# The one-hot table's weighting in the last layer of a decoder kernel moves from VectorE to GpSimd

## The reference

```
q = normalise(x @ w_q)                       # over all tokens, gamma and beta
sim = einsum("pbnhd,hkpd->pbnhk", q, keys)   # 2 halves, 8 heads, 64 keys
sx, ix = top_k(sim[0], 8);  sy, iy = top_k(sim[1], 8)
scores, pk = top_k(sx[..., :, None] + sy[..., None, :], 8)
indices = (ix * 64 + iy) picked by pk        # 8 heads x 8 picks per token
h = gelu(einsum("bnd,bnhkd->bnhk", x, down_embed[indices]))
h = softmax(scores) * h
out = einsum("bnhk,bnhkd->bnd", h, up_embed[indices])
```

## Time and profile before

| | us |
|---|---|
| median of 3 runs | 2479.22 (2472.06 to 2480.68) |
| the profiled execution, its own time | 2480.77 |
| its span in the trace | 2478.9 |
| PE busy | 1869.9 |
| DVE busy | 1342.1 |
| ACT busy | 747.7 |
| POOL busy | 243.8 |

### The profile page before, as it was taken

One profiled execution on the slowest core, in us unless ns is written; L12 is line 12 of the kernel. 1 busy time (PEld: TensorE's weight loads), 2 busy tenths in 40 slices (PEclk: granted clock), 3 DMA queues, 4 the chain that ended last, 5 costly groups with the idle time before them and its releaser, 6 DMA issues. The chain is left out here.

```text
span 2478.9 us, 35764 instructions
## 1 busy us (share of the span) xinstructions
PE 1869.9 (75%) x12618; PEld 1443.9 (58%) x12618; DVE 1342.1 (54%) x3974; ACT 747.7 (30%) x1470; POOL 243.8 (10%) x234
## 2 busy tenths in 40 slices
PE   6676776788888545887878766665878969969968
PEld 4555564656655434666666544444767757758757
DVE  3454445235433342555455534443499598697796
ACT  2231312132343323545545422230240330330420
POOL 1212212100000012000000001111010100000100
PEclk9888787867887776889888965557788989979979
DMA  2000000100000114877777511116000000000000
GB/s 84 1 17 17 0 17 0 52 6 26 25 17 1 48 55 156 295 269 279 280 249 262 189 37 34 34 34 256 9 1 1 18 1 6 14 1 6 14 1 9
DMA packets 90917, 174.74 MB, mean 70 GB/s; under 512 B 8224, under 2 KB 75296, under 8 KB 86052
## 3 DMA queue, kind: packets, MB, share of 16 engines
q1 hardware_dynamic: 90788, 173.05, 19.9%
HBM read 93.20 MB, written 79.69 MB: 70 GB/s over the span
## 5 line engine op out<-in xcount | busy, mean ns | idle before, releaser
L2122 PE MATMUL bank<-per_up,per_act_w 128*128 128x256 f32 x1024 | 256.3, 400 | 0.0
L95 PE MATMUL bank<-per_xT,per_down 128*128 128x256 f32 x1024 | 223.6, 379 | 0.0
L95 PEld LDWEIGHTS bank<-per_xT,per_down 128*128 128x128 f32 x1024 | 194.8, 190 | 33.1 <-issue 7.6
L2122 PEld LDWEIGHTS bank<-per_up,per_act_w 128*128 128x128 f32 x1024 | 194.7, 198 | 23.9
L2038 DVE TENSOR_TENSOR per_hot_x<-per_picksT,per_iota_x 128x4096 f16<-128x4096 f16 x64 | 146.0, 2281 | 0.0
L1186 DVE CUSTOM_DVE_ANT_0 rel_summed<-bank,rel_bias 128x256 f32<-128x256 f32 x256 | 97.2, 419 | 68.1 <-PE bank L1293 61.4
L1943 ACT ACTIVATE per_act_w<-bank 128x512 f32<-128x512 f32 x128 | 76.4, 597 | 162.4 <-PE bank L95 162.2
L1104 ACT ACTIVATE rel_probs<-rel_summed,rel_low 128x256 f32<-128x256 f32 x256 | 117.9, 518 | 15.5 <-DVE rel_low L1186 15.5
L2135 PE MATMUL bank<-per_hot_y,per_hot_x 128*128 128x32 f16 x2048 | 71.5, 181 | 65.4 <-DVE per_act_w L2052 55.0
L2135 PEld LDWEIGHTS bank<-per_hot_y,per_hot_x 128*128 128x128 f16 x2048 | 68.4, 99 | 85.1 <-DVE per_hot_y L2043 66.4
L724 PE MATMUL bank<-xat_kT,xat_qT 32*128 32x256 f32 x512 | 99.9, 606 | 7.9 <-DVE xat_mx L666 7.9
(11 more groups left out here) (350 smaller groups left out, 3602.4 us busy)
## 6 DMA issues: line engine op xcount, KB each, us to landing
rel_qr_rows<-rel_qr SPq DMA_DIRECT2D x32, 1024.0 KB, 6.2
rel_p_rows<-rel_probs SPq DMA_DIRECT2D x32, 1024.0 KB, 4.7
rel_bias<-rel_qr_rows SPq DMA_DIRECT2D x64, 384.0 KB, 4.3
rel_by_dist<-rel_p_rows SPq DMA_DIRECT2D x64, 384.0 KB, 4.7
per_down<-in_per_down SPq DMA_DIRECT2D x1, 4096.0 KB, 24.4
per_up<-in_per_up SPq DMA_DIRECT2D x1, 4096.0 KB, 33.6
ret_xin<-in_x SPq DMA_DIRECT2D x8, 256.0 KB, 2.7
x_after_ret<-ret_yout SPq DMA_DIRECT2D x8, 256.0 KB, 2.1
```

What stands on the lines that cost most here:

```text
L95: last = pe.matmul(dst, wt[:, c], src[:, c, :], start=c == 0, stop=c == DC - 1)
L2122: last = pe.matmul(tiles(bank[OUT_BANK[u]])[:, t, :], act_w[:, u, k, t * P:t * P + P], up[:, k, :], start=k == 0, stop=k == COLS - 1)
```

## The change

DVE only compares for hot_y, without the drain, and signals a new semaphore, hot_marked. POOL waits for it, multiplies hot_y in place by the weights and signals hot_ready, for which PE waits as before. POOL does this between its selection products and the variance of the same pass. Nothing else changes: slots, order of DVE's work, PE's waits.

```diff
@@ peer_layer
-    h_mm, gelu_ready, out_mm = sem("h_mm"), sem("gelu_ready"), sem("out_mm")
+    h_mm, gelu_ready, out_mm, hot_marked = sem("h_mm"), sem("gelu_ready"), sem("out_mm"), sem("hot_marked")
@@ POOL's stream, in the loop over passes, after the selection products
+                for u in range(2):
+                    for k in range(CHUNKS):
+                        pool.wait_ge(hot_marked, (2 * i + u) * CHUNKS + k + 1)
+                        wide = [P, CH, COLS // 4, 4]
+                        hy = hot_y[:, k % NSLOT].rearrange("p s (c e) -> p s c e", e=4)
+                        weight = picksT[:, u, 2, k * CH:k * CH + CH, :].unsqueeze(2).broadcast_to(wide)
+                        pool.tensor_tensor(hy, hy, weight, ALU.mult).then_inc(hot_ready, 1)
                 for u in range(2):
                     pool.wait_ge(var, 2 * i + u + 1)
                     pool.tensor_tensor(rs[:, u], ve[:, u], half[:, 0:2], ALU.pow).then_inc(rstd, 1)
@@ hot(i, u, k), DVE's stream
-                dve.tensor_tensor(hy, four(1, wide_y), pattern(iota_y, wide_y), ALU.is_equal)
-                dve.drain()
-                dve.tensor_tensor(hy, hy, four(2, wide_y), ALU.mult).then_inc(hot_ready, 1)
+                dve.tensor_tensor(hy, four(1, wide_y), pattern(iota_y, wide_y), ALU.is_equal).then_inc(hot_marked, 1)
```

## The result

The changed kernel takes 2500.36 us (median of 4 runs), the kernel before 2476.84 on the same chip: ratio 1.0097, 95% interval 1.0071 to 1.0123. It is slower, as forecast, but by 23.5 us where the forecast said 49 (2528 against the 2479.22 then shown). The profiled execution's span is 2502.3 us against 2478.9. As in the rows of before, pass 2 is the second of the four passes of this layer, hot_x(k) is the instruction that fills hot_x for chunk k, the compare is the one that marks hot_y, and an engine is "held" while it is kept from running an instruction that it has taken up.

The account below looks back on a forecast made before the run. DVE bounds the table work in u = 0's first half and u = 1, PE in u = 0's second half. Then POOL's multiply binds: 4.05 + 8.3 = 12.35 us a pass, four passes +49.4, giving 2528 us, range 2486 to 2600.

Parts of the forecast that it names:

- The exclusion: POOL's multiply and DVE instructions with both inputs in SBUF (hot_x, hot_y) keep each other out, whichever comes first.
- rival 1: Exclusion doesn't hold for 16-bit products; DVE runs 4.00 us a chunk beside POOL; 2472 to 2481 us; chance 0.14.
- weigh runs free: DVE's weigh has one input in PSUM, so POOL's multiply can hide behind two weighs, 1.20 us, and nothing else.
- P: Time of POOL's multiply of 1024 16-bit elements per chunk: taken as 2.4 us, bounds 1.27 and 3.6.
- The 2.2 worked out beside it: The Trainium skill's about 2.6 cycles an element at 1.2 GHz: 2.2 us for POOL's multiply, some 12 us off the sum.
- The formula for the period, 2.81 + P: Steady chunk period under exclusion: 5.2 us for P = 2.4, above DVE's 4.76 before and PE's 4.42.
- the line through a product of 512 f32 elements and one of 32: POOL's 1.271 and 0.252 us give 2.12 ns an element, so 1024 elements take 2.36 us.
- rival 3: POOL is quick, P below 1.9; at 1.9 the period is 4.71, +24 us in all; 2488 to 2503 us; chance 0.09.
- The starts: At each batch's start PE waits for POOL's first products; with the periods, u = 0 +4.05 us, u = 1 +8.3.
- The clock: At u = 1's start PE idles 6.9 us, so low clock in all four passes; unit 0 takes 4.08 us.
- The most the change could give: Multiply and drain leave DVE, 0.77 us a chunk; if only this counted, about 6 us a pass, 23 in all.
- The bounds: Range 2486 to 2600 us, leaving out rival 1 and the slowest POOL costs, under 2 in 10.

## Why the prediction was right in kind and wrong in size

A row of the kernel before that bears on the second point (L234 is a product on POOL in the retention layer):

```profile
L234 POOL TENSOR_TENSOR ret_v<-ret_v,ret_fade 128x512 f32<-128x512 f32 x8 | 8.5, 1056 | 61.7 <-DVE ret_v L330 61.7
```

- **The exclusion** was right: the f32 rows carried over to 16-bit operands, and rival 1 fell. That weigh runs free was right too. That the exclusion decides the sign is not shown, as POOL only writing, with a short read at the start, was still 0.5% slower. hot_x's mean rose to 2.61 us and not above 3, and POOL gained 141.5 us and not 154, as the product is shorter.
- **P, the cost of POOL's multiply, is the term that failed.** I took 2.4 us; it measures 1.93. The 2.2 worked out beside it is above that too. The formula for the period, 2.81 + P, gives 4.74 with it against 4.76 measured, so the steady part costs nothing instead of 0.44 us a chunk. The step that went wrong was the line through a product of 512 f32 elements and one of 32: it holds for plain f32 rows, but I carried it over to 16 bits and to a second input in repeated runs of four, which are both cheaper. The trace of the kernel before had a sign that a pattern can be cheaper, which I did not use; L234's 512 f32 elements, whose second input repeats each value, take 1056 ns and not 1271. The forecast's own text has the right answer in rival 3, "At 1.9 the period is 4.71 ... +24 in all", with 2488 to 2503 us, and gave it 9 in 100. With the price put back, the pass grows by 11.4 of the forecast 12.35 us.
- **The starts** were right in place and near in size, and that the sum with P = 1.9 (+24) comes so near the measured +23.1 is in part luck, as two misses offset each other. u = 0: rival 3's working has +1.3, the four passes +0.93, +2.07, +0.95 and +2.01. In pass 2 unit 8 starts at 23.93 instead of the 23.6 of that working, and PE's second unit ran 2.93 us at the rising clock instead of 2.45 (2055.61 to 2058.54). u = 1: rival 3's working has +4.8, the four passes +4.48, +4.09, +4.49 and +4.03. POOL slipped in between hot_x(1) and the compare, so PE's first unit came at 6.92 us, not at 7.6 (5.68 + 1.9), and in pass 2 it took 3.80 us instead of 4.08. The prediction weighed this slipping in for u = 0 alone, for the end of chunk 1's product, where it would change nothing; in u = 1 it makes unit 0 earlier.
- **The clock** at the start of u = 1 fell in all four passes, as assumed; the first unit took 3.8 to 4.0 us (forecast 4.08).
- **The most the change could give** was put at 23 us and measures 26.6 by the pass (26 to 45 by the interval of the time): u = 0 gains 4.0 instead of 3.1, u = 1 2.6 instead of 2.7.
- **The bounds**: the range of 2486 to 2600 holds the time; it was the central value that was poor.

## What to carry to other kernels

In this kernel a product on POOL was free only beside DVE's weighs, which read one input from PSUM; beside DVE instructions with both inputs in SBUF one of the two stood still. So count the time of such a cover (here two weighs, 1.20 us) and cut POOL's share to fit. Look at the start of each batch apart from the steady part: here the cover is missing, TensorE waits longest (5.75 us), and its clock falls to 0.50. And price a POOL product by a row with the same access pattern, not only the same element count.

## What was not expected of the hardware

- What a product on POOL costs depends on how its second input repeats: 512 f32 elements take 1.261 us plain and 1.057 with each value repeated 16 times; 1024 take 2.338 plain and 1.961 in repeated runs of four. Repeated runs of eight save nothing (L1923, 1.271 for 512). With the same tile as both inputs 512 take 1.04. Why is open.
- POOL, shut out by hot_x(1), got in ahead of the compare at the start of u = 1 (3.91 us from asking to end), and behind it at the start of u = 0 (4.51), in each of the four passes. In both it had asked 0.16 us after hot_x(1) began. What decides is open; no run was made for it.
